# Moving five pieces of a slot table in a fused two-layer transformer kernel

## The reference, cut to what matters

```
x  = x + L0_attn(norm(x)) + L0_ffn(norm(x))
x  = x + L1_attn(norm(x)) + L1_ffn(norm(x))

L0_attn: 16 heads of 8, rope, causal softmax with a windowed bias, then
         relu(probs + tau/row) @ v, @ Wo.  tau/row also acts on the masked
         (future) columns, so sums of v over later rows enter the result
L0_ffn:  blockwise FP4 rounding of input, weights and hidden, silu(gate) * up, down
L1_attn: linear attention: q, k = elu(rope(..)) + 1; running sums over rows of
         k v^T and of k; out = (q . kv) / max(q . ks, 1e-6), @ w_out
L1_ffn:  softmax router over 4 experts, the best 2 weighted, each
         silu(x eg) * (x eu) @ ed, plus one shared expert of the same form
```

## Time and profile before

| | |
|---|---|
| median of 3 runs | 2109.91 us (2109.56 to 2110.14) |
| the profiled execution's own time | 2108.19 us |
| its span, first to last instruction | 2106.2 us |
| mean granted TensorE clock | 0.981 of full speed |
| busy: PE, PEld | 1934.5 us (92%), 1264.0 us (60%) |
| busy: DVE, ACT, POOL | 1540.6 (73%), 1375.7 (65%), 1143.8 us (54%) |
| chain that ended last, by engine | PE 56%, ACT 16%, DVE 12%, POOL 8%, issue 7%, DMA 1% |

### The profile page before, as it was taken

How to read it: one execution, slowest core, us unless ns; L and a number is a source line. 1 busy time by engine, 2 the same in 40 slices (tenths; PEclk the granted TensorE clock), 3 DMA queues, 4 the chain that set the end, 5 groups by cost and what they waited for, 6 DMA issues and landing times.

```text
span 2106.2 us, 49813 instructions
## 1 busy us (share of the span) xinstructions
PE 1934.5 (92%) x17353; PEld 1264.0 (60%) x17353; DVE 1540.6 (73%) x5223; ACT 1375.7 (65%) x3861; POOL 1143.8 (54%) x1799
## 2 busy tenths in 40 slices
PE   3789999999999999999999999999999999998978
PEld 1455666656566575666657566575656657565645
DVE  6558778687776868778687877868777686876646
ACT  1677585675857667585766858567685766757531
POOL 4676374655637465473746647475563746545220
PEclk9779999999999999999999999999999999999999
DMA  5102021110301102020210201121030110201010
GB/s 146 27 9 44 4 39 23 34 29 8 54 4 38 24 20 42 4 56 6 39 24 18 44 4 39 23 39 24 10 52 4 38 24 17 40 4 34 4 32 6
DMA packets 172653, 59.37 MB, mean 28 GB/s; under 512 B 139643, under 2 KB 169971, under 8 KB 172403
## 3 DMA queue, kind: packets, MB, share of 16 engines
q1 hardware_dynamic: 172403, 56.19, 13.9%
HBM read 14.22 MB, written 4.19 MB: 9 GB/s over the span
## 4 chain that ended last, share of the span: by engine, by line
PE 56%; ACT 16%; DVE 12%; POOL 8%; issue 7%; DMA 1%; SPq 0%; ACTq 0%; DVEq 0%; POOLq 0%
PE ps L1124 11%; PE ps L1260 8%; PE ps L1195 8%; PE ps L1205 7%; ACT ring L946 5%; PE ps L1138 5%; PE ps L1114 4%; ACT pb L955 3%; PE ps L1245 3%; DVE ring L577 3%; PE ps L1183 2%; DVE lin L609 2%; POOL ring L843 2%; PE ps L1103 2%; PE ps L1171 2%
## 5 line engine op out<-in xcount | busy, mean ns | idle before, releaser
L843 POOL TENSOR_SCALAR ring<-ring,row_rcp,tau_row 128x128 f32<-128x128 f32 (+3 forms) x1024 | 625.5, 618 | 676.1 <-DVE row_rcp L584 676.1
L946 ACT ACTIVATE ring<-ring,neg_max 128x128 f32<-128x128 f32 (+3 forms) x1024 | 570.8, 558 | 504.0 <-DVE neg_max L577 499.4
L1124 PE MATMUL ps<-identf,ring 128*128 128x128 f32 x2560 | 378.6, 287 | 10.4 <-POOL ring L843 7.6
L955 ACT ACTIVATE pb<-ps 128x512 f32<-128x512 f32 x640 | 348.0, 583 | 27.5 <-PE ps L1124 23.2
L1124 PEld LDWEIGHTS ps<-identf,ring 128*128 128x128 f32 x2560 | 279.2, 143 | 83.4 <-issue 39.0
L577 DVE CUSTOM_DVE_ANT_1 ring<-ps,bias_t 128x384 f32<-128x384 f32 (+1 forms) x496 | 286.7, 614 | 53.7 <-PE ps L1114 46.4
L1260 PEld LDWEIGHTS ps<-ed_t,h 128*128 128x128 f32 (+1 forms) x1920 | 254.6, 191 | 97.2 <-issue 93.7
L1260 PE MATMUL ps<-ed_t,h 128*128 128x128 f32 (+1 forms) x1920 | 270.6, 277 | 0.0
L1205 PE MATMUL ps<-xn1T,eu_t 128*128 128x512 f32 (+1 forms) x480 | 256.5, 616 | 1.3 <-DVE h L633 1.2
L1195 PE MATMUL ps<-xn1T,eg_t 128*128 128x512 f32 (+1 forms) x480 | 255.6, 614 | 2.2 <-DVE h L626 2.1
L1114 PE MATMUL ps<-qkT 32*128 32x128 f16 (+3 forms) x1024 | 201.4, 308 | 47.1 <-DVE neg_max L577 28.0
(11 more groups left out here) (152 smaller groups left out, 2815.7 us busy)
## 6 DMA issues: line engine op xcount, KB each, us to landing
x_t<-x SPq DMA_DIRECT2D x16, 256.0 KB, 2.9
x<-x SPq DMA_DIRECT2D x16, 256.0 KB, 2.9
o_rows<-o_stack SPq DMA_DIRECT2D x256, 16.0 KB
out<-x SPq DMA_DIRECT2D x16, 256.0 KB, 2.3
qkT<-qkx SPq DMA_TRANSPOSE x128, 3.2
bias_t<-bias SPq DMA_DIRECT2D x1, 1536.0 KB, 7.8
eg_t<-eg SPq DMA_DIRECT2D x1, 860.0 KB
eu_t<-eu SPq DMA_DIRECT2D x1, 860.0 KB
```

The lines of the kernel that those rows point to most:

```text
L843: pool.tensor_scalar(e, e, row_rcp[:, m % 2, r:r + 1], tau_row[:, i, HG * g + r:HG * g + r + 1], ALU.mult, ALU.add).then_inc(p_ok.sem, 1)
L946: act.activation(e, e, ACT.Exp, bias=neg_max[:, n % 2, r:r + 1], scale=-1.0, accum_out=row_sum[:, n % 2, r:r + 1]).then_inc(exp_ok.sem, 1)
L955: act.activation(pb[:, c % NPB, :], bank(turn_bank(q)), ACT.Relu).then_inc(t_taken[q % 2].sem, 1)
L1124: last = pe.transpose(o[:, r * P:(r + 1) * P], ring_of(i, r)[:, k * P:(k + 1) * P], idf)
```

## The change

All of it is in the numbers at the top and in the conditions that read them. The stacks of layer 1, which came on four slots in a row (casts at 26 to 29, low parts at 27 to 30, transposes at 28 to 31), come at 27, 28, 30 and 32, with the low part one slot and the transpose two slots behind. The chunk products start at slot 37 instead of 35 and fill slot 47 too; three of the four `intra` follow. The router begins at 37 instead of 31. The down products of experts 1 and 2 go from 42 to 44 and from 48 to 49, and the accumulations of experts 0, 1 and 2 from 39, 46 and 52 to 43, 48 and 53. `fv` and `fy` go from slots 61 and 63 to 33 and 35. No instruction is added or taken away.

```diff
-TURN_H, FUTURE_V, FUTURE_Y = (ATT + 11, ATT + 13, ATT + 13, ATT + 15), ATT + 61, ATT + 63
+TURN_H, FUTURE_V, FUTURE_Y = (ATT + 11, ATT + 13, ATT + 13, ATT + 15), ATT + 33, ATT + 35
-LIN = [L1 + (35, 37, 39, 41, 43, 45, 49, 51)[v // 2] for v in range(H)]
-INTRA = (L1 + 40, L1 + 42, L1 + 46, L1 + 53)
+LIN = [L1 + (37, 39, 41, 43, 45, 47, 49, 51)[v // 2] for v in range(H)]
+INTRA = (L1 + 42, L1 + 46, L1 + 49, L1 + 53)
-ROUTER = L1 + 31
+ROUTER = L1 + 37
-DOWN1 = [GATE1[3 * e + 2] + 4 for e in range(NE - 1)] + [L1 + 65]
+DOWN1 = [L1 + p for p in (35, 44, 49, 56, 65)]
+ADD_EXPERT = [L1 + p for p in (43, 48, 53, 60, 69)]
-TURN_STACK0, TURN_STACK1 = QKV0 + 5, QKV1 + 8
+TURN_STACK0, STACK1 = QKV0 + 5, (L1 + 27, L1 + 28, L1 + 30, L1 + 32)
...
-                    if 0 <= p - TURN_STACK1 < T:
-                        turn_stack1(b, p - TURN_STACK1)
+                    if p - 2 in STACK1:
+                        turn_stack1(b, STACK1.index(p - 2))
...
-                    if p == DOWN1[e] + 4:
+                    if p == ADD_EXPERT[e]:
                         accumulate(b, e)
...
-                if 0 <= p - QKV1 - 7 < T:
-                    stack_low(b, 1, p - QKV1 - 7)
+                if p - 1 in STACK1:
+                    stack_low(b, 1, STACK1.index(p - 1))
...
-                if 0 <= p - QKV1 - 6 < T:
-                    stack_high(b, 1, p - QKV1 - 6)
+                if p in STACK1:
+                    stack_high(b, 1, STACK1.index(p))
```

## The result

| | before | after |
|---|---|---|
| median | 2110.02 us (2109.56 to 2110.74) | 2144.26 us (2143.34 to 2146.33, 4 runs) |
| ratio, 95% interval | | 1.0164 [1.0151, 1.0177] |
| span, mean granted clock | 2106.2 us, 0.981 | 2144.4 us, 0.979 |

Slower, as forecast, but by 34 us and not by 10. The mean clock is nearly the same. Between 160 and 1910 us, where the full frames stand, the granted clock stays at 2.4 GHz in the trace of after, and in that of before but for 3 to 4 us of one frame, so the time lies in the frames themselves. TensorE is busy for 1959.7 us (91%), before 1934.5 (92%); VectorE, ScalarE and GpSimd hardly changed (71, 64 and 53%).

A forecast was written before the change was run, and what follows sets the result against it. TensorE was taken to set the pace, busy 118.6 of a frame's 125 us. The terms summed to +0.7 us per frame, times 15 = +10.5 us, giving a median of 2120 us, range 2112 to 2128.

The forecast's parts named there:

- `fv` and `fy`: Slots 33, 35 and 63: 0.99 us added, TensorE 1.0 us ahead at the frame's start; 0.15 us lost per frame.
- Stacks: Slots 27 to 33: the 1.32 us stall at slot 31 stays, turning starts earlier; 0.1 us gained per frame.
- This costs 0: The last transpose lands 3.3 us after issue, 5.1 at most, in time for `lin` at slot 37; no loss.
- Rival C: `lin` at slot 37 waits for a late transpose, each us costing 15: 2135 us, chance 0.03.
- First `intra` from 40 to 42: Slot 42: the `intra`'s wait for a copy out of its bank ends; 0.3 us gained per frame.
- slot 43 loses its down tile: Slot 44: with only one `up` after `lin`, the second score waits for masking; 0.25 us lost per frame.
- The accumulation in slot 43: Slots 43 to 45: VectorE's work delays `lin`'s second head and `up` of slot 45; 0.7 us lost per frame.
- The router's other steps: Slots 37 to 42: 0.35 us per slot, hidden by VectorE's waits of 0.49 us and more for `lin`.
- A: Slot 45: VectorE is early or the accumulation covered, so 0.7 falls to about 0.1 us; 2111 us, chance 0.18.
- B: Slot 28: ScalarE starts sooner, the stall at slot 31 falls to 0.7 us; say 2100 us, chance 0.17.

The follow-up runs named there:

- two parts alone: The kernel before with only the chunk products and `intra` moved, 2166.15 us; the kernel before with only layer 1's stacks moved, 2170.95 us.

## Why the prediction was right in direction and wrong in size

The runs make a ladder from before to after. Each step is a difference of ratios, so none is better known than 4 or 5 us, and the steps of -4.6 and -2.5 aren't clear of nothing:

| step | ratio to before | us over before | this step | predicted |
|---|---|---|---|---|
| chunk products and `intra` later, expert 1 accumulated at 47 | 1.0095 | 20.0 | 20.0 | -4.5 |
| down products at 44 and 49, accumulations at 48 and 53 | 1.0073 | 15.4 | -4.6 | +3.8 |
| stacks | 1.0061 | 12.9 | -2.5 | -1.5 |
| router from 37, expert 0 accumulated at 43 | 1.0107 | 22.6 | +9.7 | +10.5 |
| `fv`, `fy` at 33 and 35 | 1.0164 | 34.6 | +12.0 | +2.3 |

The first two rows can't be set beside the prediction's terms one by one: their kernels accumulate expert 0 in slot 39, where after doesn't, and the first accumulates expert 1 in slot 47, where neither before nor after does. The terms are better read from starts in the trace of after, us per frame:

| place | predicted | read | from |
|---|---|---|---|
| stacks | -0.1 | -0.1 | scores of slot 32 to those of 34, 3.68, with `fv` and `fy` back 3.58 |
| first `intra`, slot 42 | -0.3 | -0.24 | pair to `intra`, 0.88, now 0.64 |
| slot 43 without its down tile, pair of slot 44 | +0.25 | +0.38 | pair to the next start, 0.32, now 0.70 |
| accumulation, slot 45 | +0.7 | +0.83 | `lin` to `up`, 0.33, now 1.16 |
| `fv` and `fy` | +0.15 | +0.67 | frame of after against after with them back |
| slot 35 without `lin` | none | +0.34 | gives back 0.20 of 0.54, with `fv` and `fy` back |
| other neighbours of TensorE's products | none | +0.3 | two borders more, and `pv` of slot 40 without `intra` behind it, 0.90, now 1.01 |
| sum | +0.7 | +2.2 | the frame: 127.06 less 124.87 is 2.19 |

- **`fv` and `fy`.** The mis-sized term: +0.15, measured +0.67 a frame, by the ladder 0.8. I had the 0.99 us added right, and TensorE was in fact 0.97 ahead at slots 2 and 4. What failed is the step to the norm, which "needs its shift from VectorE and GpSimd, which get only about 0.8 us earlier". Counted from the scores of slot 62, the norm did come earlier (6.84 us, before 7.35), but not the reciprocal (2.78, before 2.72), and from it start GpSimd's four scalings, which set the turning of slot 4 (8.94, before 9.03). I had named that reciprocal and followed it only to the norm. Leaving the products out of before gains 2 us, so their time was nearly free there.
- **What I had put at nothing.** Two things that the sum has no term for cost 0.6 us a frame, more than the error of the `fv` and `fy` term. A `lin` taken out of slot 35 uncovered a wait for `h` there. And "All instructions stay, so the change can only alter how long TensorE stands still" leaves out that TensorE's products take longer beside other neighbours.
- **Stacks.** Right: the stall at slot 31 stays, their place is worth 2.5 us, within the error, and in this change the transposes are in time. But "This costs 0" hid a dependence: without the later `lin` the same edit costs 61 us. Rival C had the mechanism, and only its condition was not met.
- **First `intra` from 40 to 42, slot 43 loses its down tile.** Right: 0.24 gained where I took 0.3, 0.38 lost where I took 0.25. Of the 0.38, 0.25 are there with the accumulation in slot 39 too (0.57 to the next start), and 0.13 come with it. I had said that "slot 40 held an `intra` of 1 us more, so this wait did not show", and the kernels with the accumulation still in slot 39 bear it out: the wait shows at slot 41.
- **The accumulation in slot 43.** Right in mechanism: 0.7 expected, 0.83 read at slot 45. The waits marked there (3.1 and 2.8 us) are only half of it; the rest shows in starts alone. That the ladder's +9.7 comes near the forecast 10.5 is luck: the kernel a row above loses 0.53 us at slot 41, which this step takes away again, and 1.05 less 0.53 is 0.5 us a frame, 8 us.
- **The router's other steps.** Hidden, as said, though VectorE's wait at slot 37 was 0.22 us in before and not 0.49: no wait of TensorE in slots 37 to 42 is theirs.
- **Rivals.** A and B are ruled out. Where B stood on the rule that the Trainium skill (Perfetto Trace Analysis, Optimization Strategy) gives, that interleaving the regimes of the most contended engine may help, the windows show the evening out (VectorE 7.39 to 5.77 and 5.97 to 7.24) and the time going up. The gain did not come here: the first regime's stall didn't hang on VectorE's load, and in the second TensorE had no slack to lend.

The frame of the ladder's third row adds up by the same places: 0.53 more at slot 41, 0.48 less at slot 42, 0.12 and 0.25 more at slots 43 and 44, 0.34 at slot 35, 0.3 with new neighbours, 0.1 less for the stacks, together 0.96 of 0.97. What stays open: that the neighbours cost what they do is read from starts, and no run tests it by itself. Nor does one tell why, behind the same waits, the clock fell in some frames and not in others.

## What to carry to other kernels

Price a piece of work by what it covers where it stands and by what it delays where it goes: 1 us of TensorE's time was worth 0.1 us a frame in the shade of a chain and 0.8 out of it, and a chunk product taken away uncovered a wait for another engine. Edits to such a table don't add: before trying a part alone, follow its producers and consumers (two parts alone cost 56 and 61 us, all together 35), and put long work of a serving engine behind, not ahead of, the short pieces that the bounding engine waits for. With two gates and two `intra` moved, that order made the difference between a slower version (2120.74 us) and the one that is faster than before (2098.23); alone it gave 0.15%.

## What the runs showed of the hardware

- A wait of TensorE can cost twice. After standing 2.87 us, 2.13 us, or 1.09 and 0.37 close together, its granted clock was at 1.2 GHz for 3 to 6 us; gate products took 1.9 us for 1.1. It doesn't follow each time: it did in seven of nine frames with the wait of 2.87 us, in five of ten with 1.09 and 0.37, and in four of nine with one of 1.20 us in the kernel with two gates and two `intra` moved. In before TensorE waits 1.32 us at slot 31 in nearly every frame, and the clock stays at 2.4 GHz; but in one frame it fell for 3 to 4 us behind a wait of 1.10 us at slot 28 (937.31).
- The start-to-start time of a product depends on its neighbours. Two down tiles of after, each with its successor, on TensorE:

```profile
1251.42 0.93 PE L1261 MATMUL ps<-ed_t,h 128*128 128x128 f32 x6
1252.29 0.41 PE L1172 MATMUL ps<-qkT 32*128 32x128 f16 x8
...
1293.03 0.83 PE L1261 MATMUL ps<-ed_t,h 128*128 128x128 f32 x6
1293.70 0.39 PE L1259 MATMUL ps<-wout_t,qT 128*128 128x128 f32 x2
```

  Between `intra` and chunk product it takes 0.87 us, with neither 0.67 (and 0.76 with one of them on one side, as 1246.48 to 1247.24); gate and up products show 1.06, 0.96 and 0.86 in the same way. So in these traces each border with a score, chunk or `intra` product costs 0.10 us. One frame of before has 41 such borders of these products, one of after 43: 0.2 us of the 2.2.
- VectorE's scaling of the norm's steps takes as long as GpSimd lets it. After and before, VectorE and then GpSimd:

```profile
1296.65 0.86 DVE L473 TENSOR_SCALAR x_step<-x_step 128x32 f32<-128x32 f32 x1
```

```profile
1296.68 0.79 POOL L819 TENSOR_TENSOR hid<-hid,q_step 128x352 f32<-128x352 f32 x1
```

```profile
1273.23 0.28 DVE L472 TENSOR_SCALAR x_step<-x_step 128x32 f32<-128x32 f32 x1
```

```profile
1272.68 0.78 POOL L818 TENSOR_TENSOR hid<-hid,q_step 128x352 f32<-128x352 f32 x1
```

  It ends 0.04 to 0.05 us after GpSimd's instruction both times (1297.51 after 1297.47, 1273.51 after 1273.46), once in 0.86 us and once in 0.28, and so in nine frames of each trace (0.03 to 0.05 us). In after it even starts 0.03 us ahead of that instruction, while GpSimd's scaling before it still runs (to 1296.72). The Trainium skill (Advanced Engine Details and Errata, VectorE Performance Modes) says that VectorE's second SBUF port is shared with GpSimd, and that GpSimd's instructions and VectorE's two-port ones block each other. These rows fit that; whether this instruction uses both ports no run here shows.
